# Two broadcast operations moved from VectorE to GpSimd and one cast moved to ScalarE in the normalization stage of a transformer-layer kernel

## The reference

```python
def _layernorm(x, axis=-1, eps=1e-5):
    m = jnp.mean(x, axis=axis, keepdims=True)
    v = jnp.var(x, axis=axis, keepdims=True)
    return (x - m) / jnp.sqrt(v + eps)

# _L0_attn_ref(x, ...): q, k, v = lora_linear(x, ...); softmax(q k^T * SCALE) v;
#                       lora_linear(out, Wo, bo, Bo, Ao)
# _L0_ffn_ref(x, gamma, beta, weight, bias, alpha):
    mu = jnp.mean(x, axis=-1, keepdims=True)
    var = jnp.mean(jnp.square(x - mu), axis=-1, keepdims=True)
    xn = (x - mu) * jax.lax.rsqrt(var + LN_EPS) * gamma + beta
    a = jnp.sign(xn)
    centered = weight - jnp.mean(weight, axis=1, keepdims=True)
    signed_w = jnp.sign(centered)
    out = jnp.einsum('bsi,oi->bso', a, signed_w) + bias
    return out * alpha

    xn = _layernorm(x, axis=-1)
    x = x + _L0_attn_ref(xn, ...) + _L0_ffn_ref(xn, ...)
```

## Time and profile before

| | us |
|---|---|
| median of 3 runs | 8642.88 |
| lowest and highest of them | 8490.86 and 8749.63 |
| the profiled execution | 8490.86 |
| its span, slowest core | 8489.3 |
| spans of its eight cores | 8475.6 to 8489.3 |
| PE matmul busy | 5635.1 (66%) |
| DVE busy | 3280.4 (39%) |
| ACT busy | 2489.8 (29%) |
| POOL busy | 3.7 (0%), 17 instructions |

### The profile page before, as it was taken

One profiled execution on the slowest core, in us unless ns is written; L12 is line 12 of the kernel. 1 busy time (PEld: TensorE's weight loads), 2 busy tenths in 40 slices (PEclk: granted clock), 3 DMA queues, 4 the chain that ended last, 5 costly groups with the idle time before them and its releaser, 6 DMA issues. The chain is left out here.

```text
span 8489.3 us, 69744 instructions; the slowest of 8 cores (8475.6 to 8489.3 us)
## 1 busy us (share of the span) xinstructions
PE 5635.1 (66%) x23096; PEld 2170.2 (26%) x23096; DVE 3280.4 (39%) x2910; ACT 2489.8 (29%) x2455; POOL 3.7 (0%) x17
## 2 busy tenths in 40 slices
PE   1111488888888766666666666666666665996499
PEld 0111233333333222222221221212222212332243
DVE  3666412111111244444444444444444444113433
ACT  1222100000000155555555555555555552000000
POOL 0000000000000000000000000000000000000000
PEclk9999998898989877777777777777777776997699
DMA  1111111111111100000000000000000003442344
GB/s 35 60 60 60 55 52 58 52 53 55 54 56 54 51 20 5 19 19 20 19 5 19 20 19 19 14 11 19 19 20 19 5 4 112 151 149 102 126 166 149
DMA packets 171887, 425.09 MB, mean 50 GB/s; under 512 B 26005, under 2 KB 107925, under 8 KB 142869
## 3 DMA queue, kind: packets, MB, share of 16 engines
q1 hardware_dynamic: 80922, 269.60, 9.4%
q10 hardware_dynamic: 90624, 151.02, 4.8%
HBM read 269.58 MB, written 150.99 MB: 50 GB/s over the span
## 5 line engine op out<-in xcount | busy, mean ns | idle before, releaser
L758 ACT ACTIVATE pT<-sg,negc 128x1024 bf16<-128x1024 f32 x2048 | 2095.6, 1139 | 1703.8 <-DVE ostg L594 1498.0
L768 PE MATMUL avp<-pT,vh 128*128 128x512 bf16 x4096 | 1314.4, 404 | 569.7 <-ACT pT L758 569.7
L736 PE MATMUL sg<-qT,kT 128*128 128x512 bf16 x4096 | 1290.9, 410 | 0.0
L779 DVE TENSOR_TENSOR ptree<-pT 128x4096 bf16<-128x4096 bf16 x128 | 293.4, 2292 | 1764.1 <-ACT pT L758 1764.1
L494 PE MATMUL pgB<-xn_fm,wT 128*128 128x512 bf16 x3072 | 728.1, 400 | 25.3 <-DVE wT L479 25.3
L494 PE MATMUL pgA<-xn_fm,wT 128*128 128x512 bf16 x3072 | 724.8, 398 | 25.2 <-DVE wT L479 25.2
L768 PEld LDWEIGHTS avp<-pT,vh 128*128 128x128 bf16 x4096 | 311.3, 101 | 1575.8 <-issue 1542.6
L802 DVE TENSOR_TENSOR ptree<-ptree 128x4096 bf16<-128x4096 bf16 (+3 forms) x512 | 593.4, 1159 | 64.1 <-DVE ptree L794 22.8
L736 PEld LDWEIGHTS sg<-qT,kT 128*128 128x128 bf16 x4096 | 420.3, 103 | 588.4 <-issue 169.9
L609 PE MATMUL avp<-ptree,ones_bfc 128*1 128x512 bf16 x128 | 74.8, 584 | 723.6 <-DVE obuf L606 723.6
L657 ACT ACT_TABLE_LOAD x1 | 1.3, 1283 | 1876.5 <-DMA qT<-s_qT 1876.5
(11 more groups left out here) (125 smaller groups left out, 3277.5 us busy)
## 6 DMA issues: line engine op xcount, KB each, us to landing
xf<-x SPq DMA_DIRECT2D x32, 1024.0 KB, 4.8
x_sp<-x SPq DMA_DIRECT2D x32, 1024.0 KB, 6.7
out<-res ACTq DMA_DIRECT2D x64, 512.0 KB, 3.4
ord<-out SPq DMA_DIRECT2D x32, 1024.0 KB, 6.6
out<-res4b ACTq DMA_DIRECT2D x64, 512.0 KB, 3.7
s_a<-a_acc ACTq DMA_DIRECT2D x16, 1024.0 KB, 5.1
wbuf<-wq SPq DMA_DIRECT2D x16, 1024.0 KB, 5.9
wbuf<-wk SPq DMA_DIRECT2D x16, 1024.0 KB, 5.9
```

Of the source, the lines that this page charges most:

```text
L736: ins = nc.tensor.matmul(sg3[b][:, j * 512:(j + 1) * 512], kT_b[sl][:, kt * 128:(kt + 1) * 128], qT_b[sl][:, qq0:qq0 + 512], start=True, s ...
L758: e = ac.inc(nc.scalar.activation(pT2[qsl][:, g * 1024:(g + 1) * 1024], sg3[s_bank[g]][:], AF.Exp, bias=negc2[sl].ap()))
L768: pe.inc(nc.tensor.matmul(avp[qsl][:], vh2[sl][:, kt * 128:(kt + 1) * 128], pT2[qsl][:, kt * 512:(kt + 1) * 512], start=(kt == 0), stop=(k ...
L779: tree_a[0] = dv.inc(nc.vector.tensor_tensor(ptree2[qsl][:, 0:wq // 2], pT2[qsl][:, 0:wq // 2], pT2[qsl][:, wq:wq + wq // 2], ALU.add))
```

## The change

The cast of `xn32` to `xnbf` becomes an `activation(Copy)` on ScalarE. The multiplication by gamma and the addition of beta are issued on GpSimd, with a semaphore of their own, `gpc`. The waits follow: the second normalization waits for ScalarE's copy, the sign waits for GpSimd, the transposes of `xnbf` wait for ScalarE, and from the second tile on L304's operation waits for the last GpSimd operation and the sign of the tile before.

```diff
+            gpc = S("p1_gp")
+            prev_sign = [0]
...
                 nc.vector.wait_ge(dv.h, v_nmr)
+                if t >= 1:
+                    nc.vector.wait_ge(gpc.h, gpc.v)
+                    nc.vector.wait_ge(ac.h, prev_sign[0])
                 v_xn = dv.inc(nc.vector.tensor_scalar(
                     xn32.ap(), xf[sl].ap(), stat[:, 5:6], stat[:, 6:7],
                     ALU.mult, ALU.add))
...
-                nc.vector.wait_ge(dv.h, v_xn)
-                nc.vector.wait_ge(ac.h, a_sq2)
-                v_xnbf = dv.inc(nc.vector.tensor_copy(xnbf.ap(), xn32.ap()))
+                nc.scalar.wait_ge(ac.h, a_sq2)
+                nc.scalar.wait_ge(dv.h, v_xn)
+                a_xnbf = ac.inc(nc.scalar.activation(xnbf.ap(), xn32.ap(), AF.Copy))
                 nc.vector.wait_ge(dv.h, v_nmr2)
+                nc.vector.wait_ge(ac.h, a_xnbf)
                 v_u = dv.inc(nc.vector.tensor_scalar(
                     xn32.ap(), xn32.ap(), stat[:, 5:6], stat[:, 6:7],
                     ALU.mult, ALU.add))
-                nc.vector.wait_ge(dv.h, v_u)
-                v_g = dv.inc(nc.vector.tensor_tensor(xn32.ap(), xn32.ap(), gb_g.ap(), ALU.mult))
-                nc.vector.wait_ge(dv.h, v_g)
-                v_b = dv.inc(nc.vector.tensor_tensor(xn32.ap(), xn32.ap(), gb_b.ap(), ALU.add))
-                nc.scalar.wait_ge(dv.h, v_b)
+                nc.gpsimd.wait_ge(dv.h, v_u)
+                nc.gpsimd.wait_ge(gpc.h, gpc.v)
+                gpc.inc(nc.gpsimd.tensor_tensor(xn32.ap(), xn32.ap(), gb_g.ap(), ALU.mult))
+                nc.gpsimd.wait_ge(gpc.h, gpc.v)
+                v_b = gpc.inc(nc.gpsimd.tensor_tensor(xn32.ap(), xn32.ap(), gb_b.ap(), ALU.add))
+                nc.scalar.wait_ge(gpc.h, v_b)
                 a_s = ac.inc(nc.scalar.activation(abf.ap(), xn32.ap(), AF.Sign))
+                prev_sign[0] = a_s
 
                 nhalf = min(8, NCH)
-                nc.tensor.wait_ge(dv.h, v_xnbf)
+                nc.tensor.wait_ge(ac.h, a_xnbf)
```

## The result

The changed kernel is slower. The ratio of its times to those of the kernel before is 1.0229, 95% interval 1.0164 to 1.0294, so it is clear that it is slower and not clear whether by more than 2%.

A forecast was written before the change was run, and what follows sets the result against it. Stage 1 was taken as bound by a serial chain per tile, not an engine's throughput. 0.68 + 4.42 + 0.23 = 5.33 us per tile, times 32, is 170.6 us on 8490.86: 8661 us, range 8604 to 8815.

The forecast's parts named there:

- Cast: In each stage 1 tile, ScalarE's copy following Exp starts the second normalization later: +0.68 us.
- Gamma and beta: Two POOL operations of 4.5 us in each tile's chain, 9.20 us against 4.78 on VectorE: +4.42 us.
- Hand-overs: Three slower hand-overs per tile, VectorE to POOL, POOL to POOL, POOL to ScalarE: +0.23 us together.
- Waits on things long done: Three small added waits per tile on ScalarE and VectorE, costed at nothing; otherwise 0.1 us per tile.
- Sum: The terms of one stage 1 tile together: 5.33 us, times 32 tiles 170.6 us.
- What lies beside POOL: Transposes of xnbf and the two xn_fm copies run under gamma, done under beta at the latest, adding nothing.
- POOL at its memset's pace (1): Gamma and beta on POOL take 1.80 us each: -0.07 us per tile, 8489 us; chance 0.05.
- Table loads (3): Copy lacks stage 1's activation table, so each tile loads tables twice: 82 us, 8743 us; chance 0.06.
- Rival 5: Gamma and beta on POOL take over 5.4 us each: 8720 us and more, 9064 at 10.8; chance 0.06.
- P: Length of one POOL operation for gamma or beta: 4.5 us, the middle between 3.6 and 5.4.
- Rival 4: POOL and VectorE hold each other up, gamma waiting for the xn_fm copies: 44 us, 8705 us; chance 0.03.
- Rival 2: Tiles overlap, the next tile's sum and square running under POOL: -30 us, 8461 us; chance 0.02.

The follow-up runs named there:

- e1: The kernel before with only the cast moved to ScalarE: pitch 26.62 us a tile, time 8512.47 us against 8491.30 on the same chip.
- e4: The changed kernel without the two waits added ahead of the first normalization: stage 1 1002.5 us, 5.0 less; its total can't be compared.
- e6: The changed kernel's placement (cast on ScalarE, gamma and beta on GpSimd) put into e5: pitch 19.65 us, lowest run 8308.27 us.
- e5: The kernel before, placement kept, with sign, transposes and copies issued later and xn32 double: pitch 21.22 us, time 8350.24 us, ratio 0.9823.
- e8: e7 with the cast back on VectorE: pitch 17.14 us, stage 1 569.2 us; its totals can't be compared.
- e7: e6 with the first normalization moved to ScalarE: pitch 17.73 us, stage 1 587.5 us, lowest run 8239.18 us.

## Why the prediction was right about the kernel and wrong about the number to compare

**Where it was wrong.** 8661 us is the time that the four lowest runs give (8659.17 to 8661.81), but the median over all runs is 8781.92. The point that I gave stood only 18 us over the median shown for before (8642.88), and so read as no change, while the median moved by 144 us and the ratio is 1.0229. The step that failed is the last of the sum: it was made against the profiled execution's 8490.86, one of the lowest runs, and not carried to the median, although the text had the difference (152 us) and the result (8813). The medians of after and before stand 121 and 148 us above the means of their four lowest runs. Carried over, the forecast would have been 8813, 31 us off. The range, which reached there, held it. That my sum and 2% were the same size made it a coin's toss whether the kernel would be over 2% slower; the measurement leaves it undecided as well.

**The terms, by after's timeline against the earlier trace rows.**

- *Cast:* from Exp's start to the second normalization's start 1.62 us before (515.84 to 517.46), 2.16 after (494.58 to 496.74): +0.54, forecast +0.68. The copy starts 0.14 us after Exp's start, inside it, not behind it. That start, 0.15 us earlier than forecast, is the whole of the difference. e1 gives 0.57.
- *Gamma and beta:* 4.50 and 4.49 us, forecast 4.5. From gamma's start to the sign's 9.22 us (498.29 to 507.51), forecast 9.20 without slower hand-overs. The choice between 3.6 and 5.4, which carried most of the sum, came out at its middle; that was luck as far as rows go, since no row of before decided it.
- *Hand-overs:* POOL starts 1.55 us after the second normalization's start, VectorE's gamma 1.45: +0.10. POOL to POOL 0.14, POOL to ScalarE 0.09. Together +0.13 over VectorE's 0.10 each (0.10 for the start, 0.04 and -0.01 inside the 9.22), forecast +0.23.
- *Waits on things long done:* +0.14 a tile (0.46 against 0.32 before L309's operation), costed at nothing, with 0.1 as the bound. I had read the price off the cast, whose two satisfied waits have no live one ahead of them; those before L304's operation do. e4 shows that it is the waits.
- *Sum:* 0.54 + 4.44 + 0.10 + 0.14 = 5.22 a tile; measured 5.24; forecast 5.33. Two terms too high, one missing.
- *What lies beside POOL:* right. The `xn_fm` copies run at 498.00, 0.29 us ahead of gamma's start, and at 498.85, both done under gamma and 0.69 us long.

**The rivals.** POOL at its memset's pace (1) fell: 4.5 us. Table loads (3) fell; after has six, one in each block, as before, and none in the tiles:

```profile
L256 ACT ACT_TABLE_LOAD x1 | 1.3, 1283 | 111.3 <-DVE stat L250 111.3
L440 ACT ACT_TABLE_LOAD x1 | 1.3, 1283 | 14.4 <-PE pgA L434 14.4
```

With the rule of the Trainium skill (ScalarE: Activation LUTs, section Table sets) that copy is in every set the trace agrees: Copy (L317) follows Exp and the sign follows Copy with one load for the whole stage. Rival 5 fell with P. Rival 4, that the two engines hold each other up, did not occur in the change: POOL's gamma starts while an `xn_fm` copy is running. But it is real, as e6 shows, for another operation, and it waits for whoever lets the tiles overlap. Rival 2, overlap, did not occur either; e5 to e8 show what it takes. My sum for it (30 us gained) assumed one `xn32` and the change's waits, and was not tried in that form.

## What to carry to other kernels

In a stage bound by a chain, moving work to an idle engine changes the time by the difference of the two durations, not by the busy time set free: look first at what the freed engine would do meanwhile, and in which order its queue lets it. Here the slow engine paid only once something ran beside it, so change the order first (0.982 with the placement untouched) and the placement after, and then look in the trace for instructions that grew longer beside it. And when the profiled execution stands well under the median of the runs shown, say on which of the two the forecast is made.

## What the runs showed of the hardware that I had not expected

- A VectorE f32 `tensor_scalar` of 128x2048 that starts while GpSimd runs a `tensor_tensor` lasts 3.8 to 4.2 us instead of 1.35 and ends 1.08 to 1.09 us after GpSimd's (e6). The lost time is in the instruction's own duration. Row sums, copies out of PSUM and ScalarE's activations are not lengthened (e7).
- A satisfied wait behind a live one cost VectorE 0.07 us (none 0.32, one 0.39, two 0.46 us from start to start, in e4, e5 and after); the two satisfied waits ahead of the cast cost nothing that shows.
- ScalarE's copy begins 0.14 us after the start of the 0.20 us Exp ahead of it, when it does not need its result (after, e1).
- GpSimd's `tensor_tensor` of 128x2048 f32 took 4.49 to 4.52 us in after, e6 and e7, and a dependent one starts 0.14 us after the end of the first.
- By the trace, eight transposes of 128x128 bf16 took 1.01 to 1.06 us at a granted TensorE clock of 1.00 (before) and of 0.50 (e5).
